# Two weighing visits per head group merged into one, and the divisions moved forward, in a four-layer cross-attention and feed-forward kernel

## What is computed

```
# block 0
scores = einsum('bhsd,bhtd->bhst', q, k) / sqrt(16)
scores = clip(scores, -50, 50); masked = -10000, clipped to -50
probs = softmax(scores); ctx = probs @ v; delta = ctx @ Wo.T + bo; layernorm, residual
# block 2: 8-bit quantised q and output projections around
attn = softmax(q @ k.T / sqrt(16)); o = attn @ v
# block 3: two softmaxes over two parts of the context (257 and 255 rows), summed
out = (softmax(q @ k_img.T) @ v_img + softmax(q @ k.T, masked) @ v) @ Wo + bo
```

## Time and profile before

| | |
|---|---|
| median of 3 runs | 1154.88 us |
| span of the profiled execution | 1153.3 us |
| fastest run, 0.9 us above that span | 1154.19 us |
| PE / PEld / DVE / ACT / POOL busy | 88 / 66 / 70 / 49 / 37% of the span |
| mean granted TensorE clock | 0.949 |

### The profile page before, as it was taken

How to read it: one execution, slowest core, us unless ns; L and a number is a source line. 1 busy time by engine, 2 the same in 40 slices (tenths; PEclk the granted TensorE clock), 3 DMA queues, 4 the chain that set the end, 5 groups by cost and what they waited for, 6 DMA issues and landing times.

```text
span 1153.3 us, 19199 instructions
## 1 busy us (share of the span) xinstructions
PE 1015.4 (88%) x6456; PEld 764.3 (66%) x6456; DVE 807.4 (70%) x1639; ACT 570.5 (49%) x1129; POOL 431.4 (37%) x519
## 2 busy tenths in 40 slices
PE   4899868989877998789999875899999989998998
PEld 3566547877766877565664664566555568887887
DVE  6477758678866668688886765877675266776766
ACT  3788754444433442236667442265655534444443
POOL 5524414355303455523220324323210134554553
PEclk8999989899998999879999988899999889999999
DMA  6936624454320478754520336736511134455554
GB/s 180 249 93 155 124 72 128 143 162 132 121 92 1 128 135 204 167 93 121 126 53 21 118 75 142 149 88 94 122 34 31 49 109 126 155 151 152 159 156 122
DMA packets 82059, 136.43 MB, mean 118 GB/s; under 512 B 11565, under 2 KB 40518, under 8 KB 79546
## 3 DMA queue, kind: packets, MB, share of 16 engines
q1 hardware_dynamic: 71034, 101.93, 29.9%
q0 software_dynamic: 10944, 33.45, 17.1%
HBM read 113.41 MB, written 22.97 MB: 118 GB/s over the span
## 4 chain that ended last, share of the span: by engine, by line
PE 59%; DVE 17%; DMA 6%; issue 6%; ACT 6%; POOL 4%; SPq 1%; DVEq 0%; ACTq 0%; POOLq 0%
PE psum L616 36%; PE psum L909 7%; PE psum L876 6%; PE psum L885 5%; DMA ff_raw<-in_ff 4%; ACT probs L1058 2%; DMA weights_out<-combine 1%; DVE nmx L1371 1%; DVE nmx L1374 1%; DVE ff_s L1997 1%; DVE nmx L1372 1%; PE psum L835 1%; POOL ff_wl L1958 1%; DVE probs L1465 1%; PE psum L717 1%
## 5 line engine op out<-in xcount | busy, mean ns | idle before, releaser
L616 PE MATMUL psum<-ff_xh,ff_wh 128*128 128x512 f32 x424 | 176.8, 417 | 22.3 <-POOL ff_wl L1958 17.6
L2014 DVE TENSOR_TENSOR ff_hl<-ff_h,ff_hh 128x512 fp32r<-128x512 f32 x114 | 121.9, 1069 | 94.5 <-ACT ff_hh L1899 94.1
L1958 POOL TENSOR_TENSOR ff_wl<-ff_raw,ff_wh 128x512 fp32r<-128x512 f32 x92 | 120.6, 1311 | 171.7 <-ACT ff_wh L1910 171.4
L1060 ACT ACTIVATE probs<-psum 128x512 f32<-128x512 f32 x256 | 144.1, 597 | 78.8 <-PE psum L876 75.1
L876 PE MATMUL psum<-queries,keys 128*128 128x512 f32 x384 | 155.7, 436 | 12.9 <-ACT probs L1058 6.1
L616 PE MATMUL psum<-ff_xh,ff_wl 128*128 128x512 f32 x392 | 156.7, 400 | 0.0
L1910 ACT ACTIVATE ff_wh<-ff_raw 128x512 fp32r<-128x512 f32 x92 | 58.0, 630 | 181.9 <-DMA ff_raw<-in_ff 179.1
L616 PE MATMUL psum<-ff_wh,ff_hh 128*128 128x256 f32 x456 | 131.1, 291 | 9.3 <-DVE ff_hl L2014 9.2
L885 PE MATMUL psum<-keys,queries 128*128 128x512 f32 x256 | 118.2, 478 | 18.6 <-DVE nmx L1372 8.3
L616 PE MATMUL psum<-ff_wh,ff_hl 128*128 128x256 f32 x456 | 129.9, 289 | 0.0
L1963 POOL TENSOR_TENSOR ff_wl<-ff_raw,ff_wh 128x256 fp32r<-128x256 f32 x92 | 91.3, 992 | 61.7 <-ACT ff_wh L1917 60.6
(11 more groups left out here) (263 smaller groups left out, 2199.5 us busy)
## 6 DMA issues: line engine op xcount, KB each, us to landing
ff_w<-weights_out SPq DMA_DIRECT2D x94, 256.0 KB
ff_raw<-in_ff SPq DMA_DIRECT2D x92, 256.0 KB, 3.6
ff_raw<-in_ff SPq DMA_DIRECT2D x106, 128.0 KB, 2.1
keys_out<-keys_turned SPq DMA_DIRECT2D x24, 512.0 KB, 3.7
keys<-keys_out POOLq DMA_DIRECT2D x48, 256.0 KB, 5.1
queries_out<-queries_turned SPq DMA_DIRECT2D x24, 256.0 KB, 4.3
keys<-keys_out POOLq DMA_DIRECT2D x48, 128.0 KB, 5.4
queries<-queries_out POOLq DMA_DIRECT2D x32, 192.0 KB, 4.0
```

The costliest lines, as they stand in the source:

```text
L616: last = eng.matmul(dst, lhs[i](k), rhs[j](k), start=start and n == 0, stop=stop and n == groups * len(pairs) - 1, skip_group_check=True)
L1060: ins = eng.activation(dst, src, ACT.Exp, scale=SCALE)
L1958: then(eng.tensor_tensor(ff_wl[:, slot, 0:2 * D], raw(n, slot)[:, 0:2 * D], ff_wh[:, slot, 0:2 * D].bitcast(F32), ALU.subtract), "f_w1r")
L2014: then(eng.tensor_tensor(ff_hl[:, slot, :], ff_h[:, slot, :], ff_hh[:, slot, :].bitcast(F32), ALU.subtract), "f_hr")
```

## The change

Both parts of a group are weighed at one position, the last unit of the second part plus `PAIR_AFTER` (3.4 in block 0, 2.6 in blocks 2 and 3). Before, each part had its own position (5.6, 7.8 and 4.6 units after its own last unit). So in block 0 the first part's weighing moves from 1.6 units after the group's last score to 3.4, and the second's from 5.6 to 3.4; in block 2 from 3.8 and 7.8 to 2.6; in block 3 from 0.6 and 4.6 to 2.6. In blocks 2 and 3 the transposes `dt` and divisions `dd` of a batch move forward by 2.8 and 3 units. `SUM_AFTER` still sets the point from which the steps after a batch are counted.

```diff
-    2: [("dt", 0, 1.8), ("dd", 0, 2.4), ("dt", 1, 4.4), ("dd", 1, 4.4), ("ot", None, 13.3), ("oe", None, 13.8),
+    2: [("dt", 0, -1), ("dd", 0, -.4), ("dt", 1, 1.6), ("dd", 1, 1.6), ("ot", None, 13.3), ("oe", None, 13.8),
...
 SUM_AFTER = {0: 5.6, 2: 7.8, 3: 4.6}
+PAIR_AFTER = {0: 3.4, 2: 2.6, 3: 2.6}
...
-            at(r + 4 * part + 3 + lag + SUM_AFTER[blk], "wg", c, part)
             if part % 2:
-                at(r + 4 * part + 3 + lag + SUM_AFTER[blk] + MISC["ev"], "ev", c, part // 2)
+                both = r + 4 * part + 3 + lag + PAIR_AFTER[blk]
+                at(both, "wg", c, part - 1)
+                at(both, "wg", c, part)
+                at(both + MISC["ev"], "ev", c, part // 2)
```

## The result

| | before | after |
|---|---|---|
| median of the runs shared on one chip | 1154.54 us (4 runs) | 1194.26 us (4 runs) |
| range | 1151.26 to 1156.72 | 1189.62 to 1195.37 |
| span of the profiled execution | 1153.3 us | 1191.4 us |
| mean granted TensorE clock | 0.949 | 0.947 |
| block 0, first to last exponential's start | 114.1 us | 134.7 us |

The change makes the kernel 3.4% slower: ratio 1.0343, 95% interval 1.0315 to 1.0372. The forecast was 1164 with a range to 1173. So the direction was right, and the loss was 40 us where I had 9. The direction comes from block 0 alone: blocks 2 and 3, where I had a gain, lost too.

The account below looks back on a forecast made before the run. TensorE was taken to pace blocks 2 and 3, while in block 0 scores and exponentials wait in turn. +15 - 3.2 - 2.8 = +9 us on 1153.3 gives 1162.3, plus 1.6 makes 1164 us; range 1150 to 1173.

Parts of the forecast that it names:

- Price and count of changes: All three blocks: 93 visits become 48, each saved change of column groups worth .32 us, 14.4 us of TensorE time.
- The pair lasts 6.9 instead of 5.42: Block 0: a pair takes 1.5 us more, as the second part waits for the clip and ScalarE idles.
- 10 intervals x 1.5 = 15 us: Block 0: of 15 intervals between pairs, ten lose 1.5 us each; bounds -4.8 to +22 us.
- x .32 = 3.8 us I take 3.2: Block 2: 12 pairs of batches 0 to 2 save .32 us each, 3.2 us counted as gain; batch 3 counts 0.
- TensorE paces: Block 2: TensorE, busy 94.1 of 96 us, sets the pace; no separate size.
- No new wait stands at the visit: Block 2: with two score banks, scores ahead of the visit already waited for the group's last exponentials; no added wait.
- the starving of VectorE: Blocks 2 and 3: longer visits leave VectorE without maxima; at .1 us for each of 30 visits, 3 us lost.
- 15 x .32 = 4.8 at most: Block 3: 15 saved changes give at most 4.8 us; 2.8 us counted as gain.
- The earlier dt and dd at 0: Blocks 2 and 3: moving these transposes and divisions forward changes no count and costs 0 us.
- TensorE as the pace of block 0: Rival: block 0 gains and loses nothing, 1149 us, or all 45 changes come off, 1140 us; chance .13.
- half: Rival: in block 0 projections absorb the wait except in the barest groups, 7.5 us lost against -6, 1156 us; chance .13.
- The clock: Rival: TensorE's granted clock falls in block 0, costing about 5 us, 1169 or 1174 us; chance .12 (clock or worse).

Follow-up runs that it names:

- The run at 5.4: Against the kernel before: joined visits in block 0 alone, 5.4 units after the group's last score; 1164.39 us, ratio 1.0075.
- apart at 2.6: Kernel after with block 0 as before and, in blocks 2 and 3, a separate early visit for each part; 1164.76 us, ratio 1.0089.

## Why the prediction was right and where it failed

*Price and count of changes: right.* There are 48 visits, of x32 in blocks 0 and 2 and x40 in block 3, and a pair is cheaper by .23 us on TensorE where nothing else binds (.32 by my sum). What was wrong is to book it as time.

*"The pair lasts 6.9 instead of 5.42": right* in size, 6.71, and in its place: the wait for `probs` stands ahead of the second half and ScalarE idles behind it. The reason given was half the truth. I wrote that it could not happen before because the second part stood behind five scores. The run at 5.4 has almost that (four scores) and still loses .75 in a bare pair, as three banks do not outlast the visit.

*Block 0, "10 intervals x 1.5 = 15 us": mis-sized.* It measured 20.6, of which up to 2.5 can be the clock's: 18.1 against the kernels in the old order with as much time at half clock, and 19.3 (134.1 for 114.6 to 114.9) by the same rule in the kernel with pairs in block 0 alone. The ten intervals that I counted lost 17.0 us, 1.7 each: 1.0 to 2.0 in eight, and 2.7 in the two behind the first groups of batches 1 and 2, where the clip stands behind the divisions. Of the five that I left out, the two behind the second groups of batches 1 and 2 lost nothing, as forecast; the one behind the first group of batch 3 lost 2.1, the first of all .8 and the last .3. About 4 us go with half a clip and as much with the place 5.4 (14 us over the old order stay in each, at like clock), some 5 more with the length of the exponentials, and 9 stay when they are short too.

*Block 2, "x .32 = 3.8 us I take 3.2", a gain: this step failed.* It measured a loss of 10.5 (1.5 of it in batch 3, which I had at 0): 7.8 by the place of the visits (131.1 apart at 2.6 for 123.3), 2.6 by joining them there. "TensorE paces" was read from 94.1 of 96 us. But VectorE's 84.7 stood beside it, and ScalarE waited 18.8 us: I now read it as three in-order queues with two or three banks between them, in step, none of which paces alone. The runs fit that and do not prove it. The sentence "No new wait stands at the visit" was true of the scores and beside the point: the new waits are VectorE's and ScalarE's during the visit, and TensorE's own some 3 us behind its end (it begins at 605.12 in the trace above). I had named the starving of VectorE and priced it at .1 us a visit; in the trace above it is 1.50 us, and then 1.15 more on TensorE. The move to an earlier place, for which I looked only at whether the visit's inputs are ready, I had priced at 0, and it is three quarters of this block's loss. Which collision makes which place dear is open. That VectorE is a party to it is shown for the kernel after (6.8 of 10.4 us go with short maxima). The projection and dd were tested as the other party and are not in the main.

*Block 3, "15 x .32 = 4.8 at most", of which 2.8 taken as a gain: failed too.* A loss of 5.4: at like clock about 3.7 by the place and 1.7 by joining there, though at the old place joining costs 4.7. It does not go with the length of VectorE's maxima, as short ones leave 6.1. That its visits are longer (40 rows) and its score banks are two fits, but no run shortened a visit, so it is argued and not shown.

*The earlier dt and dd at 0: right in sum*, .5 us in block 2 and none in block 3, with 2.4 to 2.7 us moved between neighbouring groups.

*The rivals.* TensorE as the pace of block 0 and "half" are out. The clock came in a small way: granted .97 over 48 to 182 us for 1.00 over 47 to 158 before, and .50 around one visit (the granted clock is the third number from the right):

```profile
162.90:165.50 2.60, 2.60 (x27) 1.08 (x30) 2.19 (x4) 1.50 (x3) 0.00 (x0) 0.50 0.00 0
```

Such stretches come in block 0 of the old order too, up to 10.2 us of them, so the change is not shown to cause them. The kernel with pairs in block 0 alone takes 134.1 us with 3.4 us of them, the kernel after 134.7 with 10.2; the clock is at most 2.5 of the 20.6 us. I had priced the clock's fall at about 5 us; as the comparison above shows, 10.2 us at half clock go with 2.5 in block 0 of the old order. No rival had blocks 2 and 3 slower, so the range ended at 1173 while the bounds that I had written for them ended at 3 us lost.

## What to carry to other kernels

A busy share of 98% on one engine does not make work saved on it into time, when a neighbour with in-order work stands at 88% and only two or three banks lie between them: look at what each engine has in stock when the saved work is gone, and for how long. Joining two short absences of an engine into one long one can cost more than it saves once the long one outlasts the stock (in block 0 three scores at .575 us against 1.87 us). A step that is moved is priced at its new place as well: where engines run in step, ask what each of them does at that moment and not only whether the step's inputs are ready. And before a few microseconds of one trace are put down to a change, look whether the granted clock was the same in both.

## What was unexpected

The place of the visits alone moves block 2 by up to 9.6 us of 123 (7.4 outside the group slowed by the clock), more than all saved changes of the array's mode could give (3.8 to 5 us), and it turns the sign of joining. With half the clip, block 0 in the old order changes by .6 us (some 1.2 at like clock), and with a quarter of each maximum block 2 by .5, though VectorE then has 68.2 instead of 84.6 and 66.2 instead of 100.1 us of work there: under an order in step that work was nearly free.
